# Float32r parts for the shared down projection, with moved gates, moved loads and another order of the down weights

## The reference, cut to what matters

```python
# x, ctx: (8, 256, 512)
x = x + attention(layernorm(x), ctx)       # 16 heads of 16 channels, over 512 positions
ht = rmsnorm(layernorm(x)).reshape(2048, 512)
probs = softmax(ht @ router_w)             # 8 experts
topv, topi = top_k(probs, 2)               # weights normalised over the two
w_dense = zeros((2048, 8)); w_dense[t, topi] = topv
g, u = ht @ w_gate[e], ht @ w_up[e]        # every expert: 512 -> 256
moe = sum_e w_dense[:, e] * ((silu(g) * u) @ w_down[e])      # 256 -> 512
sh = (silu(ht @ sw_gate) * (ht @ sw_up)) @ sw_down           # the shared expert
out = x + moe + sh                         # all in float32
```

## Time and profile before

| what | value |
|---|---|
| median of 3 runs | 837.06 us |
| the profiled execution | 836.97 us |
| its span | 835.0 us |
| TensorE busy | 790.5 us, 95% |
| VectorE busy | 533.0 us, 64% |
| ScalarE busy | 413.4 us, 50% |
| GpSimd busy | 363.5 us, 44% |
| mean granted TensorE clock | 0.987 |

### The profile page before, as it was taken

One profiled execution on the slowest core, in us unless ns is written; L12 is line 12 of the kernel. 1 busy time (PEld: TensorE's weight loads), 2 busy tenths in 40 slices (PEclk: granted clock), 3 DMA queues, 4 the chain that ended last, 5 costly groups with the idle time before them and its releaser, 6 DMA issues. The chain is left out here.

```text
span 835.0 us, 11637 instructions
## 1 busy us (share of the span) xinstructions
PE 790.5 (95%) x3843; PEld 390.2 (47%) x3843; DVE 533.0 (64%) x1006; ACT 413.4 (50%) x758; POOL 363.5 (44%) x309
## 2 busy tenths in 40 slices
PE   7999999999999999999999999998999999999993
PEld 2434334334334343343343455865555555555552
DVE  5787888898888888878888667668722222222221
ACT  2115667767777677687775774220422332233321
POOL 4207427417328155182123321000137777777774
PEclk9999999999999999999999999899999999999997
DMA  8956475566665765566533236410935655556553
GB/s 277 213 120 195 99 161 132 123 138 143 145 136 126 159 152 129 133 132 155 121 80 121 95 111 243 173 51 27 357 99 97 100 90 97 98 97 99 91 95 44
DMA packets 54185, 109.66 MB, mean 131 GB/s; under 512 B 12200, under 2 KB 27304, under 8 KB 49888
## 3 DMA queue, kind: packets, MB, share of 16 engines
q1 hardware_dynamic: 37080, 79.39, 37.5%
q0 software_dynamic: 16960, 29.37, 18.5%
q10 hardware_dynamic: 88, 0.16, 0.1%
HBM read 67.90 MB, written 40.86 MB: 130 GB/s over the span
## 5 line engine op out<-in xcount | busy, mean ns | idle before, releaser
L1053 DVE TENSOR_REDUCE negmax<-front_ps 128x1 f32<-128x512 f32 x512 | 326.7, 685 | 70.3 <-PE front_ps L903 68.7
L803 ACT ACTIVATE probs<-st_ps 128x512 f32<-128x512 f32 x512 | 284.7, 598 | 152.2 <-PE st_ps L937 135.5
L1323 POOL DMA_INDIRECT out<-x_sb,row_i x78 | 122.0, 1564 | 67.8 <-ACT x_sb L1373 54.7
L1530 PE MATMUL big_ps<-w_gu,attn 128*128 x312 | 140.4, 593 | 1.9 <-DMA w_gu<-in_gate_up 1.9
L1730 DVE TENSOR_TENSOR zeros<-attn,big_ps 128x256 f32<-128x256 f32 x39 | 16.4, 422 | 117.4 <-ACT attn L1385 117.4
L640 POOL CAST early<-early 128x512 fp32r<-128x512 f32 x28 | 17.1, 612 | 167.3 <-ACT early L756 167.3
L1530 PEld LDWEIGHTS big_ps<-w_gu,attn 128*128 128x128 f32 x312 | 56.2, 190 | 58.0 <-issue 58.0
L1385 ACT ACTIVATE attn<-big_ps 128x256 f32<-128x256 f32 x39 | 15.0, 384 | 118.7 <-PE big_ps L1530 118.7
L937 PE MATMUL st_ps<-stacks 50*128 50x512 f32 x256 | 68.5, 493 | 2.2 <-ACT probs L803 2.0
L1306 POOL DMA_INDIRECT x_sb<-h_rows,row_i x39 | 39.6, 1016 | 69.7 <-DMA out<-x_sb 58.2
L950 PE MATMUL pv_ps<-probs,early 128*32 128x512 f32 x512 | 68.5, 607 | 0.3 <-ACT probs L803 0.2
(11 more groups left out here) (204 smaller groups left out, 1140.8 us busy)
## 6 DMA issues: line engine op xcount, KB each, us to landing
parts_dram<-early SPq DMA_DIRECT2D x32, 512.0 KB, 4.4
stacks<-parts_dram SPq DMA_DIRECT2D x32, 256.0 KB, 5.3
w_gu<-in_gate_up SPq DMA_DIRECT2D x8, 1024.0 KB, 13.1
x_sb<-in_x SPq DMA_DIRECT2D x8, 512.0 KB, 9.7
early<-in_ctx POOLq DMA_DIRECT2D x8, 512.0 KB, 5.4
stacks<-parts_dram SPq DMA_DIRECT2D x32, 128.0 KB, 5.7
k_stack<-parts_dram SPq DMA_DIRECT2D x16, 256.0 KB, 4.4
q_stack<-parts_dram SPq DMA_DIRECT2D x16, 256.0 KB, 5.3
```

The costliest lines, as they stand in the source:

```text
L803: nc.scalar.activation(probs[:, k % 2, u % GH, :], score_bank(UNITS * s + u), ACT.Exp, scale=SCALE).then_inc(exp_done, 1)
L1053: nc.vector.tensor_reduce(negmax[:, n % 2, c:c + 1], smax_bank(UNITS * n + u), AX_X, ALU.max, negate=True).then_inc(max_done, 1)
L1323: nc.gpsimd.indirect_dma_start(outs[i], bass.IndirectOffsetOnAxis(ap=row_i[:, k:k + 1], axis=0), y_sb[:, k % RING, DY * i:DY * (i + 1)], N ...
L1530: mm = nc.tensor.matmul(gu_ps[:, :], h_t[:, k % 2, a, :], w_gu[:, bass.ds(expert, 1), a, :], start=(a == 0), stop=(a == DT - 1))
```

## The change

The shared down projection is made of float32r parts: each of its two float32 products a tile becomes three float32r products (high by high, high by low weight, low by high weight). For this ScalarE casts the shared down weights once and each of the eight activations (`cut_act`), and VectorE subtracts to get the low parts (`split_act`, and once for the weights). The high parts of the activations of group g lie where the cast down weight of expert g will be.

- TensorE: gates of piece 2 and the logits of tiles 12 to 15 now alternate; `shared_gates(7)` stands ahead of the places' product; two products of zeros stand at the end of the attention block.
- VectorE: `shared_act(3)` moves behind more of the counting; `shared_act(6)` and `(7)` move ahead of `shared_add(6)` and `(7)`, and those behind `row_i`.
- SyncE: `w_gu[0]` after all gates; the down weights in the order 0, 1, 4, 5, 6, 7, 2, 3, the first ahead of the stores of tiles 6 and 7, the others behind them.
- ScalarE: the cast of the first down weight waits for 8 tiles of the shared down projection, that of expert 2 for all 16.
- In the attention block `row_stats_of` moves one step behind `residual`, and the chain of the reciprocal root in half 14 is spread further.

The diff, cut to its core:

```diff
@@ attention block
+                for _ in range(2):
+                    nc.tensor.matmul(st_ps[:, 0, 0:F], zeros[:, 0:P], zeros[:, 0:F], start=True, stop=True)
                             residual(dve, out_batch(s), ended_at(late_units(s), u), proj_ps[:, :])
-                            row_stats_of(out_batch(s), ended_at(late_units(s), u))
+                            if s == HALVES - 1:
+                                row_stats_of(out_batch(s), ended_at(late_units(s), u))
+                        if s < HALVES - 1 and out_batch(s) is not None and ended_at(late_units(s), u - 2) is not None:
+                            row_stats_of(out_batch(s), ended_at(late_units(s), u - 2))
...
@@ token block, memory
+        sh_act_low = act_parts[:, :].rearrange("p (g c t) -> p g c t", c=FT, t=T)
+        sh_act_high = [down_high[:, FT * T * g:FT * T * (g + 1)].rearrange("p (c t) -> p c t", t=T) for g in range(GROUPS)]
+        sh_dn_high, sh_dn_low = attn_low[:, 1, :, :], xn_high
+        DOWN_ORDER = (0, 1, 4, 5, 6, 7, 2, 3)
@@ sync
-                for t in range(2 * RING):
+                for t in range(GT):
+                    store_base(t)
+                sp.wait_ge(shgu_ready, FT * GROUPS)
+                sp.dma_start(w_gu[:, 0, :, :], gate_up[0]).then_inc(wgu_loaded, 16)
+                for t in range(GT, GT + 2):
                     store_base(t)
                 sp.wait_ge(found_ready, 1)
...
@@ scalar
+                act.wait_ge(y_ready, CT * B)
+                nc.scalar.activation(sh_dn_high, sh_dn[:, :, :], ACT.Copy).then_inc(shdn_cut, 1)
+                cut_act(0)
+                cut_act(1)
                 silu(2)
...
+                for i, e in enumerate(DOWN_ORDER):
                     act.wait_ge(wdn_loaded[e], 16)
+                    if i == 0:
+                        act.wait_ge(shdn_ready, 2 * GT)
+                    if e == 2:
+                        act.wait_ge(shdn_ready, NTILE)
@@ tensor, shared_down(t)
+                        for i, (a, w) in enumerate(((high, sh_dn_high), (high, sh_dn_low), (low, sh_dn_high))):
+                            mm = nc.tensor.matmul(tr_ps[:, t % 2, :], a, w[:, c, :], start=(c == 0 and i == 0),
+                                                  stop=(c == FT - 1 and i == PRODUCTS - 1))
@@ tensor
-                shared_gates(2, (0,))
-                for t in range(EARLY, NTILE):
-                    logits(pe, t)
-                shared_gates(2, (1,))
+                for i in range(CT):
+                    shared_gates(2, (i,))
+                    for t in range(EARLY + CT * i, EARLY + CT * (i + 1)):
+                        logits(pe, t)
...
                 shared_down(GT + 1)
+                shared_gates(7)
                 pe.wait_ge(places_ready, 1)
...
-                shared_gates(7)
@@ vector, behind the last operation ahead of the places' product
                 shared_add(4)
                 shared_add(5)
+                split_act(4)
+                split_act(5)
+                shared_act(6)
...
-                shared_add(6)
-                shared_add(7)
-                shared_act(6)
+                shared_act(7)
+                split_act(6)
                 dve.wait_ge(found_ready, 1)
...
-                shared_act(7)
+                shared_add(6)
+                shared_add(7)
+                split_act(7)
```

More of the change, by code:

```diff
@@ L401, in row_stats, with row_variance @@
             chained(dve, last)
-        def row_variance(dve, lo, hi, scale=1.0, eps=LN_EPS):
-            for t in range(lo, hi):
+        def row_variance(dve, lo, hi, scale=1.0, eps=LN_EPS, first=None):
+            for t in range(lo if first is None else first, hi):
                 last = nc.vector.bn_aggr(mv[:, t, :], stats[:, t, :])
@@ L1125, in _ @@
                             dve.wait_ge(xn_ready, B)
-                            token_variance(dve, 0, EARLY)
+                            for t in range(EARLY // 2):
+                                nc.vector.bn_aggr(mv[:, t, :], stats[:, t, :])
                         if s == HALVES - 2 and u == 2:
+                            row_variance(dve, 0, EARLY, 1.0 + RMS_EPS, LN_EPS * RMS_EPS, EARLY // 2)
+                        if s == HALVES - 2 and u == 4:
                             rstd_guess(dve, 0, EARLY)
-                        if s == HALVES - 2 and u in (4, 6, 8):
-                            rstd_step(dve, 0, EARLY, (u - 4) // 2)
+                        if s == HALVES - 2 and u in (6, 8, 10):
+                            rstd_step(dve, 0, EARLY, (u - 6) // 2)
                         e = early_step(s, u)
@@ L1276, in store_base @@
                                      ).then_inc(base_first if t < 2 * RING else base_rest, 16)
-                for t in range(2 * RING):
+                for t in range(GT):
[3 more added lines that the diff above has]
+                for t in range(GT, GT + 2):
                     store_base(t)
                 sp.wait_ge(found_ready, 1)
-                for e in range(KEPT):
+                for i, e in enumerate(DOWN_ORDER):
                     sp.dma_start(w_dn[:, e, :, :], down[e]).then_inc(wdn_loaded[e], 16)
-                sp.wait_ge(shgu_ready, FT * GROUPS)
-                for e in range(KEPT, E):
-                    sp.dma_start(w_dn[:, e, :, :], down[e]).then_inc(wdn_loaded[e], 16)
-                sp.dma_start(w_gu[:, 0, :, :], gate_up[0]).then_inc(wgu_loaded, 16)
+                    if i == 0:
+                        for t in range(GT + 2, 2 * RING):
+                            store_base(t)
                 for t in range(2 * RING, NTILE):
@@ L1354, in _ @@
                 for j in range(3, FT * GROUPS):
+                    if j < FT * GROUPS - 1:
+                        cut_act(j - 1)
                     silu(j)
-                for e in range(E):
+                cut_act(FT * GROUPS - 2)
+                cut_act(FT * GROUPS - 1)
+                for i, e in enumerate(DOWN_ORDER):
                     act.wait_ge(wdn_loaded[e], 16)
+                    if i == 0:
+                        act.wait_ge(shdn_ready, 2 * GT)
+                    if e == 2:
+                        act.wait_ge(shdn_ready, NTILE)
                     nc.scalar.activation(w_dn_high[:, e, :, :], w_dn[:, e, :, :], ACT.Copy).then_inc(wdn_high, 1)
@@ L1585, in _ @@
                 rows_low(dve, 2, everything, DT + 2)
+                dve.wait_ge(shdn_cut, 1)
+                V.tensor_tensor(sh_dn_low[:, :, :], sh_dn[:, :, :], sh_dn_high.bitcast(F32), ALU.subtract).then_inc(shdn_split, 1)
+                split_act(0)
+                split_act(1)
                 def by_expert(ap):
@@ L1614, in _ @@
                 shared_add(3)
+                split_act(2)
                 dve.wait_ge(cnt_ready, 1)
@@ L1645, in _ @@
                 chained(dve, V.tensor_tensor(POS, POS, cnt_ps[:, 0, :, :], ALU.add))
+                shared_act(3)
                 for c, m in enumerate((M1, M2)):
@@ L1673, in _ @@
                 chained(dve, V.tensor_tensor(vals[:, :, 4], wf[:, 1, :], vals[:, :, 3], ALU.subtract))
+                split_act(3)
                 dve.wait_ge(shgu_ready, 2 * FT)
@@ L1704, in _, with split_down @@
                 V.tensor_scalar(row_i[:, :], found[:, 0, :], dump[:, 0:1], None, ALU.add).then_inc(row_ready, 1)
-                shared_act(7)
-                def split_down(e):
-                    dve.wait_ge(wdn_high, e + 1)
+                shared_add(6)
+                shared_add(7)
+                split_act(7)
+                def split_down(i, e):
+                    dve.wait_ge(wdn_high, i + 1)
                     V.tensor_tensor(w_dn_low[:, e, :, :], w_dn[:, e, :, :], w_dn_high[:, e, :, :].bitcast(F32),
                                     ALU.subtract).then_inc(wdn_low, 1)
-                for e in range(E):
-                    shared_add(NTILE - E + e)
-                    split_down(e)
+                for i, e in enumerate(DOWN_ORDER):
+                    shared_add(NTILE - E + i)
+                    split_down(i, e)
                 def turn_copy(k):
```

21 lines of the change are left out of this document (17 added, 4 removed).

## The result

The changed kernel took **842.04 us** (median of 4 runs, 841.24 to 845.61) against 837.08 of the kernel before: ratio 1.007, 95% interval 1.0039 to 1.01. Forecast were 837.8, range 833.3 to 841.3. Timed again with 12 runs (`r_after`) it took 840.20 against 836.67, ratio 1.005 (1.0026 to 1.0074). So it is 3.5 to 5 us slower by the medians, 4.2 to 5.9 by the ratios, and the forecast of "about the same" is wrong. The ratios leave out one run among all, the longest of h_zero (846.41 us), which the rule for slow runs (over 1.5% above the kernel's fastest) takes out.

What follows compares the result with a forecast made beforehand. It followed the chain up to the block loop's first gate product at 606.05 us (TensorE 95% busy). From 836.97 us, attention block -3.5, loop start +2.35 and clock +2.0 gave +0.85: 837.8 us, range 833.3 to 841.3.

Steps and rivals of the forecast that it cites:

- Attention block, -3.5: Attention block: stalls of half 13 -1.2, clock fall at 450 -0.8, zero products -1.5; together -3.5 us.
- The -1.5 for the zero products: End of the attention block: two zero products keep the clock up, so last_half takes 1.8 us, not 3.63; -1.5 us.
- Token block, first half: Logits through the places' product: new order and shorter products put the end of that product at 582.2 instead of 581.0 us.
- the forecast's 1.2: Token block, places' product: found at 582.2 us instead of 581.0, so later.
- 2.8 if the clock stays: Token block, behind the logits: 12 gates that took 5.26 us at half clock take 2.8 at full clock.
- VectorE's wait: Token block, second half: shared_act(6) waits for eight shared_down tiles, VectorE idle 7 to 8 us; row_i 589.1 instead of 586.9.
- The third rival: Token block: the wait for eight tiles doesn't hold VectorE, loop start -2.5 us, in all 833.0 us; chance 0.10.
- The +2.35: Block loop's start: first gate product at 608.4 us, 2.35 later than 606.05; bounds -2.5 and +3.5.
- The clock, +2.0: Falls behind new idle time: 1.0 at 542.6, 0.7 before the loop, 0.3 at the logits; +2.0 us, bounds 0 and +5.1.
- The slower rival: Behind 542.6 and before the loop: clock falls decide against the change, +4.35, 841.3 us; chance 0.30.
- the loads' 16.66 us: Down loads before the loop: upper bound +3.5 us if they take the eighth load's 16.66 us instead of 15.4.
- two falls of 2.5: Clock behind the new idle stretches: upper bound +5.1 us, from two falls of 2.5 each.

Runs made afterwards that it cites:

- h_zero: The kernel before with only the two zero products behind the last pv: 837.24 us against 836.49, ratio 1.0008.
- b_att: The kernel before with all the attention block's edits alone (later row statistics, later and spread rstd chain, two zero products): 833.68 us against 836.28.
- d_stats: The kernel before with one edit, the row statistics two units later: 833.72 us against 836.28.
- c_tok: The changed kernel without the attention block's edits: 841.57 us against 836.28 of the kernel before, ratio 1.0072.
- r_norstd: The changed kernel with the rstd chain of before, the other edits kept: 840.39 us.
- r_fillonly: The changed kernel with three zero products on TensorE between the first turned tokens and the loop's first gate product: 839.77 us.
- f_tokonly: c_tok with VectorE's block numbers, copy of found, row_i and adds of tiles 6 and 7 ahead of shared_act(6) and (7): 837.31 us, ratio 1.0013.
- j_copy: g_loads with the adds of tiles 8 to 15 ahead of most down-weight splits, and the turned tokens' copy ahead of the last two casts: 830.57 us, ratio 0.9933.
- g_loads: f_norstd with the seven down loads ahead of the stores of tiles 6 and 7, gathers waiting for the stores of tiles 0 to 3 alone: 835.11 us.
- f_norstd: The changed kernel with VectorE's found copy, row_i and adds ahead of shared_act(6) and (7), and the rstd chain of before: 833.60 us.

## Why the prediction was wrong

- **Attention block, -3.5: half right.** The stalls of half 13 went. Measured on before it is -1.9 (b_att), -2.8 (d_stats), and the clock is higher over their runs. The -1.5 for the zero products is the first term that failed: h_zero +0.7 (interval -1.6 to +2.9), its mean clock that of before. I read one execution's fall at 510 as if it belonged to the program; in c_tok and d_stats it wasn't there without any edit to it.
- **Token block, first half: the order right, the size taken from a bad yardstick.** This is the second term that failed. The new idle time at tile 2 was 2.42 us (2.9 forecast), 1.12 in r_after, and the places' product came with no wait ahead of it. Its start behind `last_half` was 69.19 in before; less 1.7 for `last_half`, with the forecast's 1.2 added, that gives 68.7; measured were 68.3 to 70.3. But the forecast had half clock behind the logits in the kernel before and full clock in the changed one ("2.8 if the clock stays"). The same token block of before, in the profiles of b_att and d_stats, has the product 64.4 and 65.9 us behind `last_half`, where before's 69.19 less the 1.7 would be 67.5: b_att's had no fall behind the logits, d_stats' a shorter one. Against these two the changed block is 2.4 to 5.9 us later there, not 1.2. How often the fall comes in before isn't on record, so how much of the missing time this is stays open.
- **VectorE's wait: the right step, and its own price right.** VectorE idle 7.68 us (7 to 8 forecast), TensorE 4.90 (4.8 forecast), the seven loads 12.4 us behind the start of the places' product (12.0 by the forecast's 591.3 and 582.2 less 2.94). The third rival, the case without the wait, lay 4.85 us under the forecast (-2.5 against +2.35); measured are 4.1 and 4.9, give or take some 3. The +2.35 itself was short by what follows the loads: the last of the seven had its cast begin 16.55 us behind their issue (592.59 to 609.14; 16.50 in r_after, 16.54 in r_norstd) where the prediction took 15.4 and had 16.66 only as its bound. That and loads 1.3 us later than forecast make the loop's first gate product 2.4 us late (610.82 against 608.4).
- **The clock, +2.0.** In the profile of after it fell at 545, 590 and 610. Behind the 4.9 us of idle time it fell in all five profiles that have them (after, r_after, r_norstd, r_fillonly, c_tok), which the prediction left out as covered by the loads. The fall at 610 cost 2.8 us (6.51 against 3.70) and 1.7 in r_after; the prediction had 0.7. Against it the prediction set the 2.47 us at 576 with 1.00; b_att's profile has the same idle time at the same product with a fall (4.54 us instead of 2.94):

```profile
571.17 4.54 PE L1477 MATMUL cnt_all<-rows_or_down 128*128 128x195 bf16 x32 [2.47 <-DVE rows_or_down L1693]
```

- **The sum.** Forecast: -3.5 for the attention block, +4.35 for the token block and the clock behind it. Measured: -1.9 by b_att, and -1.8 by c_tok against r_after; +6.0 by c_tok (ratio 1.0072). Both parts were off by 1.6 us, and both towards too fast; each measured part is uncertain by some 2 us, and by d_stats the attention block is off by 0.7 alone. The slower rival's 841.3 was the better time. Its reason, that the clock decides, is a part of it only: about 0.8 us of r_after's loss goes with the clock, and the zero products before the loop, which hold the clock there, left r_fillonly as slow as r_after. That its number fits is in part luck. Two bounds of the prediction are a tenth off: the loads' 16.66 us give +3.6, two falls of 2.5 give +5.0; nothing rests on them.
- The rule that I weighed, of the page TensorE: Matmul & The Clock Gate of the Trainium skill, section on a second HAM failure mode (frequent short gaps make the clock go down and up again), doesn't say here which gap brings a fall. 1.82 us at 462 came with 0.73 and 0.50 in after, 1.5 us at the same place with 1.00 in r_after, the same program. And the stall of 0.75 us at half 13, with 0.72 in before, came with 1.00 in c_tok, the same attention block.

What stays open: when the clock falls. Profiles of one and the same program differ by a fall or two, and the profile's one execution doesn't say how often.

## What to carry to other kernels

When an edit turns a buffer over to a new reader, look where the writer's wait now stands in its engine's program: one wait for a tile that comes late, ahead of small operations that release loads, cost 4 to 5 us, and moving it behind them took no wait away. When a forecast starts from one profile, ask which of its clock falls belong to the program: compare a second profile of the same stretch, or the mean clock of many runs, before one of them is counted as something to gain. Follow the chain from the loads to the very last operation that its engine does before the consumer, not to the last load. And shorter products brought nothing here that 12 runs could tell (f_tokonly); ask first what else stands on the path to the loads.

## What was not expected of the hardware

- Executions of one kernel differ more than an edit is worth: d_stats took 830.56 to 835.78 us in 12 runs at mean granted clocks of 0.994 to 0.986, the shortest at 0.994, the two longest at 0.988 and 0.986.
- The DMA engines moved 407 GB/s in j_copy and 406 in g_loads between 584 and 596, with loads, stores and gathers together. g_loads' seven loads left some 4 us earlier than f_norstd's, but the sixth weight's cast began at 595.73 against 595.95: only who goes first had changed.
